# Orders of a step on four queues: normalising ahead of W's parts, squares and root ahead of the last parts of x1, statistics ahead of low parts, all quarter loads on SyncE

## The reference, cut to what matters

```python
# L0: adapter with layernorm, weights picked by language id
h = relu(x @ W1[lang] + b1[lang])            # 512x512 @ 512x128
y = x + h @ W2[lang] + b2[lang]              # 512x128 @ 128x512
mean = jnp.mean(y, axis=-1, keepdims=True)
var = jnp.mean(jnp.square(y - mean), axis=-1, keepdims=True)
normed = (y - mean) * jax.lax.rsqrt(var + LN_EPS)
x1 = x + normed * gamma[lang] + beta[lang]
# L1: linear, weights picked by category id
out = x1 + x1 @ W[cat] + b[cat]              # 512x512 @ 512x512
```

## Time and profile before

| | |
|---|---|
| median of 3 runs | 616.76 us |
| profiled execution, its own time | 616.09 us |
| its span | 614.3 us |
| TensorE busy | 607.1 us, 99% |
| VectorE, ScalarE, GpSimd busy | 523.2, 512.8, 524.0 us |
| HBM read and written | 132.17 and 33.55 MB |
| granted TensorE clock | 1.0 |

### The profile page before, as it was taken

One profiled execution on the slowest core, in us unless ns is written; L12 is line 12 of the kernel. 1 busy time (PEld: TensorE's weight loads), 2 busy tenths in 40 slices (PEclk: granted clock), 3 DMA queues, 4 the chain that ended last, 5 costly groups with the idle time before them and its releaser, 6 DMA issues.

```text
span 614.3 us, 10766 instructions
## 1 busy us (share of the span) xinstructions
PE 607.1 (99%) x2888; PEld 492.3 (80%) x2888; DVE 523.2 (85%) x1154; ACT 512.8 (83%) x769; POOL 524.0 (85%) x262
## 2 busy tenths in 40 slices
PE   9999999999999999999999999999999999999998
PEld 7767888888877888888888888888888888888887
DVE  1799899889799898898988998888898988998673
ACT  4768889889888889888989889889888989889770
POOL 4789999899889899889999888898988999888830
PEclk9999999999999999999999999999999999999999
DMA  9968998897997988989888998988998888998422
GB/s 308 247 206 272 307 305 275 278 296 250 307 297 251 301 271 281 318 270 292 274 287 280 306 297 258 287 280 273 313 290 280 281 287 275 300 306 276 154 85 104
DMA packets 125759, 166.24 MB, mean 271 GB/s; under 512 B 10882, under 2 KB 72588, under 8 KB 121632
## 3 DMA queue, kind: packets, MB, share of 16 engines
q1 hardware_dynamic: 94756, 150.12, 75.2%
q10 hardware_dynamic: 30972, 15.78, 9.2%
HBM read 132.17 MB, written 33.55 MB: 270 GB/s over the span
## 4 chain that ended last, share of the span: by engine, by line
PE 93%; DMA 2%; ACT 2%; DVE 2%; issue 1%; SPq 0%; POOL 0%; DVEq 0%; POOLq 0%; ACTq 0%
PE o_bank L828 18%; PE o_bank L830 18%; PE o_bank L829 18%; PE n_bank L846 9%; PE d_bank L828 5%; PE d_bank L830 5%; PE d_bank L829 5%; PE d_bank L859 5%; PE y_bank L828 2%; PE y_bank L830 2%; PE y_bank L829 2%; DMA x_tok<-in_x 2%; ACT norm L491 1%; PE y_bank L836 1%; DVE xT L659 1%
## 5 line engine op out<-in xcount | busy, mean ns | idle before, releaser
L828 PE MATMUL o_bank<-w_hi,x1T_hi 128*128 128x512 f32 x512 | 205.3, 401 | 0.8 <-DVE x1T_lo L724 0.8
L830 PE MATMUL o_bank<-w_hi,x1T_lo 128*128 128x512 f32 x512 | 200.0, 391 | 0.0
L829 PE MATMUL o_bank<-w_lo,x1T_hi 128*128 128x512 f32 x512 | 199.1, 389 | 0.0
L418 POOL TENSOR_TENSOR w_lo<-w_raw,w_hi 128x1024 fp32r<-128x1024 f32 x62 | 149.4, 2409 | 9.9 <-ACT w_hi L501 9.9
L659 DVE STREAM_TRANSPOSE xT<-x_quad 128x512 f32<-128x512 f32 x120 | 127.2, 1106 | 31.1 <-DMA x_quad<-in_x 31.1
L491 ACT ACTIVATE norm<-y,neg_mean_rstd,rstd 128x512 f32<-128x512 f32 x127 | 151.1, 1264 | 1.1 <-DVE neg_mean_rstd L709 1.1
L413 POOL TENSOR_TENSOR x_tok<-x_tok,b_bc 128x1024 f32<-128x1024 f32 x60 | 145.4, 2424 | 1.2 <-issue 1.1
L830 PEld LDWEIGHTS o_bank<-w_hi,x1T_lo 128*128 128x128 f32 x512 | 96.1, 188 | 21.0
L508 ACT ACTIVATE x1T_hi<-n_bank,params 128x512 fp32r<-128x512 f32 x126 | 84.6, 689 | 33.6 <-DVE n_bank L718 26.4
L828 PEld LDWEIGHTS o_bank<-w_hi,x1T_hi 128*128 128x128 f32 x512 | 96.3, 188 | 19.6 <-issue 1.7
L829 PEld LDWEIGHTS o_bank<-w_lo,x1T_hi 128*128 128x128 f32 x512 | 96.4, 188 | 17.8
(11 more groups left out here) (87 smaller groups left out, 821.2 us busy)
## 6 DMA issues: line engine op xcount, KB each, us to landing
w_raw<-in_L_cond_W SPq DMA_DIRECT2D x32, 1024.0 KB, 6.5
out<-out_half SPq DMA_DIRECT2D x63, 512.0 KB, 4.1
x_tok<-in_x SPq DMA_DIRECT2D x31, 1024.0 KB, 11.3
w_raw<-in_L_cond_W SPq DMA_DIRECT2D x64, 256.0 KB, 4.1
b_bc<-in_L_cond_b SPq DMA_DIRECT2D x64, 256.0 KB, 8.5
x_quad<-in_x SPq DMA_DIRECT2D x62, 256.0 KB, 3.7
x_quad<-in_x ACTq DMA_DIRECT2D x58, 256.0 KB, 10.7
x_tok<-in_x ACTq DMA_DIRECT2D x2, 256.0 KB, 3.3
```

The costliest lines, as they stand in the source:

```text
L418: pool.tensor_tensor(w_lo[q][:, c:c + 2, :], w_raw[q][:, c:c + 2, :], w_hi[q][:, c:c + 2, :].bitcast(F32), ALU.subtract).then_inc(w_lo_don ...
L828: pe.matmul(acc, lhs_hi, rhs_hi, start=first, stop=False)
L829: pe.matmul(acc, lhs_hi, rhs_lo, start=False, stop=False)
L830: return pe.matmul(acc, lhs_lo, rhs_hi, start=False, stop=last)
```

## The change

The order of the lists changes on four queues, and one issuer changes. No amount of arithmetic or of data changes.

- ScalarE: three of the four `normalise` now stand ahead of `high_w(k, 0)`, and the fourth ahead of `high_w(k, 2)`. W2's high part moves ahead of `relu`. The high parts of x and W1 of the next sample move from behind `high_x1` 0 and 1 to ahead of them. The fourth square and the root move ahead of `high_x1` 2 and 3. The DMA issue of two quarters goes.
- VectorE: `variance` and `inverse_deviation` move ahead of `low_x1` 2 and 3.
- GpSimd: the first sum with b2 moves ahead of `plus_identity`, the second ahead of the first low part of W; the low part of x stands ahead of that of W1.
- SyncE: all four quarters are loaded here. The parameters of sample k, not k+1, are now copied in step k, behind the load of x, and half 1 of sample k-3 is stored there.

```diff
 # SyncE, step
+                if w_load and k.since(2):
+                    lang_now = sample_id(0, k.sample(0), L)
                 if quads:
                     sp.wait_ge(xT_done, k.count(NC, 0, NC))
                     load_x_quads(k.sample(-2), p)
...
                 if loads:
                     load_b2(lang, q)
                     load_x(k.sample(-1), q)
+                if w_load and k.since(2):
+                    sp.wait_ge(x1_lo_done, k.count(NC, 1, 0))
+                    load_params(lang_now, p)
+                if linear and k.since(3):
+                    store(k, 3, 1)
                 if turn:
...
                     load_b(cat_b, q)
                 if linear:
                     store(k, 2, 0)
-                if loads:
-                    sp.wait_ge(x1_lo_done, k.count(NC, 0, 0))
-                    load_params(lang, q)
-                if linear:
-                    store(k, 2, 1)
 # GpSimd, step
+                    if adapter and not k.last(2):
+                        plus_b2_pair(0)
                     if turn:
                         plus_identity()
-                    if adapter:
+                    if adapter and k.last(2):
                         plus_b2_pair(0)
-                    if turn:
-                        low_w_pair(0)
                     if adapter:
                         plus_b2_pair(2)
                     if turn:
+                        low_w_pair(0)
                         low_w_pair(2)
                 if follow:
                     low_w2(q, k.count(1, -1, 1))
                     if k.since(2):
+                        low_xs(k)
                         low_w1(k)
-                        low_xs(k)
 # ScalarE, step
-                    high_w(k, 0)
-                    for t in range(NT):
-                        normalise(k, t)
+                for t in range(NT - 1):
+                    normalise(k, t)
+                high_w(k, 0)
+                normalise(k, NT - 1)
                 high_w(k, 2)
+                if follow:
+                    high_w2_of_next(k)
                 if adapter:
                     relu(k)
-                if follow and not k.last(S - 2):
-                    load_next_x_quads(k)
+                if follow:
+                    high_xs_of_next(k)
+                    high_w1_of_next(k)
                 high_x1(k, 0)
                 high_x1(k, 1)
-                if follow:
-                    high_w2_of_next(k)
-                    high_w1_of_next(k)
-                    high_xs_of_next(k)
                 if adapter:
-                    square(k, 0)
-                    square(k, 1)
-                    square(k, 2)
+                    for t in range(NT):
+                        square(k, t)
+                    deviation(k)
                 high_x1(k, 2)
                 high_x1(k, 3)
-                if adapter:
-                    square(k, 3)
-                    deviation(k)
 # VectorE, step
                 x1(k, 2)
                 x1(k, 3)
+                if adapter:
+                    variance(k)
+                    inverse_deviation(k)
                 low_x1(k, 2)
                 low_x1(k, 3)
                 output(k, 3)
-                if adapter:
-                    variance(k)
-                    inverse_deviation(k)
```

More of the change, by code:

```diff
@@ L234, in sample_id, with load_x_quads @@
                 return sp.value_load(ids[0:1, which, bass.ds(s, 1)], min_val=0, max_val=count - 1)
-            def load_x_quads(s, p, quads=(0, 1)):
-                for n in quads:
+            def load_x_quads(s, p):
+                for n in range(NQ):
                     sp.dma_start(x_quad[p][quad(n), :, :],
@@ L336, in _ @@
             load_params(lang1, 1)
-            load_x_quads(2, 0, range(NQ))
+            load_x_quads(2, 0)
             step(0, 1, linear=False)
@@ L350, in _ @@
             last = Step(S // ROUND, 3)
+            store(last, 3, 1)
             store(last, 2, 0)
@@ L547, in step @@
                 k = Step(h, p)
-                if k.last(2):
-                    for t in range(NT):
-                        normalise(k, t)
-                    high_w(k, 0)
-                else:
-                    high_w(k, 0)
-                    for t in range(NT):
-                        normalise(k, t)
+                for t in range(NT - 1):
+                    normalise(k, t)
+                high_w(k, 0)
+                normalise(k, NT - 1)
                 high_w(k, 2)
+                if follow:
+                    high_w2_of_next(k)
                 if adapter:
                     relu(k)
-                if follow and not k.last(S - 2):
-                    load_next_x_quads(k)
+                if follow:
+                    high_xs_of_next(k)
+                    high_w1_of_next(k)
                 high_x1(k, 0)
                 high_x1(k, 1)
-                if follow:
-                    high_w2_of_next(k)
-                    high_w1_of_next(k)
-                    high_xs_of_next(k)
                 if adapter:
-                    square(k, 0)
-                    square(k, 1)
-                    square(k, 2)
+                    for t in range(NT):
+                        square(k, t)
+                    deviation(k)
                 high_x1(k, 2)
                 high_x1(k, 3)
-                if adapter:
-                    square(k, 3)
-                    deviation(k)
-            def load_x_quads(s, p):
-                for n in (2, 3):
-                    act.dma_start(x_quad[p][quad(n), :, :],
-                                  x_quads[bass.ds(s, 1), n].rearrange("o j b f -> j (o b) f")
-                                  ).then_inc(xq_in[p], 16)
-            def load_next_x_quads(k):
-                act.wait_ge(xT_done, k.count(NC, 0, NC))
-                load_x_quads(k.sample(-2), k.b)
             act.dma_start(x_tok[0][:, 1, :], x_rows[0, :, 1, :]).then_inc(first_x_in[1], 16)
@@ L627, in _ @@
             high_w2_of_next(k1)
-            load_next_x_quads(k1)
             for p in range(2, 2 + ROUND):
```

## The result

The changed kernel takes 751.11 us (median of 4 runs, 748.37 to 754.19) against 616.63 us of the kernel before on the same chip: a ratio of 1.2173, 95% interval 1.2149 to 1.2197. The profiled execution took 749.55 us, its span is 747.7 us. Forecast were 711 us in a range of 675 to 750: the sign and the mechanism came out, the size did not.

A forecast was written before the change was run, and what follows sets the result against it. TensorE bound the old kernel; the copy behind SyncE's loads would set a 21.3 us period. relu(3) at 77.0, 27 periods, a 19.7 step, 36.6 to the end: 708.4; plus 1.8 is 710.5, said as 711 us, range 675 to 750.

The forecast's parts named there:

- the landing term of loop B: SyncE's queue, W1's issue to x landed: 2.88 MB at 319 GB/s plus 1.9 us, 10.9 us (bounds 10.1 to 13.4).
- loop B: relu, squares, SyncE's loads, parameters landing behind x, next relu: period 21.3 us (20.5 to 23.8), deciding; chance 0.84.
- The fixed part of the term: SyncE's loads: landing time beyond bytes over rate, 1.9 us, the middle of 2.3 and 1.5.
- the undiscounted row of 13.4 us: Kernel before: x landed 13.4 us behind W1's issue while about 1.05 MB of quarters moved; taken as upper bound.
- rival 1: SyncE: the small copy passes the loads or the queue isn't served in order; only loop A, 659.5 us; chance 0.10.
- Loop A: ScalarE and VectorE: low part of chunk 2 ready at 12.4 behind relu, due 11.1; period 19.7 us.
- Where TensorE waits: TensorE waits 2.9 us in each step, partly at down for hT_lo, mostly at chunk 2.
- rival 2: TensorE's clock falls in the waits; 923 us if half of each step ran at 1.2 GHz; chance 0.04.
- The rest, costed at nothing: ScalarE's norms and W parts, GpSimd's order, quarter loads and half 1's store fit within the longer step, adding nothing.
- rival 3: Hand-over to linear tile 0: chunk 2's low part stays within 1.1 us slack, copy not late; 615 us; chance 0.02.

The follow-up runs named there:

- h1: The changed kernel with W loaded by four DMAs of 128x512 in pieces of 2 KB instead of one with 8 KB pieces: 755.05 us.
- e9: The kernel before with one change, all four quarters of x issued by SyncE and none by ScalarE: 626.77 us, ratio 1.0171.
- g1: The changed kernel with the parameter copy directly behind W1 and W2 and the store of half 1 behind it, both ahead of W, b2 and x: 654.85 us.
- e10: The kernel before with three normalise ahead of W's parts and GpSimd's order of the change: 633.48 us, ratio 1.0277.
- e6: The kernel before with squares, root and statistics ahead of the last high and low parts of x1: 643.34 us, ratio 1.0439.
- e5: The kernel before with the high parts of the next W2, W1 and x ahead of the first two high parts of x1: 680.69 us, ratio 1.1047.
- f1: The changed kernel with the parameter copy directly behind the loads of W1 and W2, the half store left in place: 667.37 us, ratio 1.0814.
- g2: g1's kernel with the high parts of the next x and W1 back behind the first two high parts of x1: 629.65 us, ratio 1.0215.
- h2: The changed kernel with W's load issued ahead of the wait for the squares and of W1's load: 686.17 us, ratio 1.1119.

## Why the prediction was wrong in size and right in kind

**The failed step is the landing term of loop B,** "How long from the issue of W1 until x has landed", 10.9 us = 2.88 MB at 319 GB/s plus 1.9. Measured are 12.4 on average and 13.4 in the step shown (383.24 to 396.6), inside the bounds that I gave (10.1 to 13.4). From relu(3) at 77.20 to relu(30) at 691.47 are 27 turns of 22.75, where 21.3 was forecast. 27 times 1.45 us is 39 us, and 710.5 + 39 = 749.5 is the profiled execution; the other terms cancel to within half a microsecond.

The fixed part of the term, 1.9 us, held: W1 lands 2.7 behind its issue, just as 0.26 MB at 319 GB/s and 1.9 us give. What failed is the one rate for all that follows. W and b2 took 6.1 us for the 4.1 that it gives them, and x 2.7 for its 3.3. I took the mean rate from a stretch in which another issuer's quarters kept the DMA engines full; in the changed kernel the queue is empty when W1 is issued. Why W and b2 are slow there stays open. The form of W is excluded by h1, and both are fast in e9.

**The range failed with it.** Its upper end, 750, allowed 1.4 us more a step, a landing of 12.3; the mean was 12.4. I had set aside the undiscounted row of 13.4 us, in which x landed behind W1 in the kernel before. It would have forecast a turn of 23.8, too long by 1 us.

**Loop B as a mechanism:** right. relu(2) at 53.88 (55.7 forecast), relu(3) at 77.20 (77.0; luck, since a start 1.8 us too late and a turn 2.0 too short met), from relu(31) to the end 36.7 (36.6), squares done and W1 issued 10.27 behind relu (10.3). The queue serves in order, which rival 1 denied: the copy lands 0.3 us behind x, and in 1.7 us when only W1 and W2 stand ahead. The section "Queues, rings and completion order" of the Trainium skill, "DMA: Bandwidth & Descriptors", says the same of a ring; the trace agrees with 10.7 us against 3.0.

**Loop A:** right, but loop B covers it in this kernel up to the last turn, relu(30) to relu(31), 19.52 us. g1 shows it in all steps: 19.56 us a step (19.7), chunk 2 taken 12.25 behind relu (12.4), 654.85 us for the kernel with nothing else in its way.

**Where TensorE waits:** I said mostly at chunk 2. It waits 1.85 at down and 0.59 at chunk 2. The period isn't touched by that, only by relu.

**The clock (rival 2)** fell, and cost nothing where a run can show it. Behind the wait of 1.85 us at down the windows read 0.63 and 0.52, the lower of the two levels for most of the time, and a matmul of 128x512 takes 0.43 us instead of 0.23. But the first square comes 7.07 behind relu in this kernel and 7.08 in g1 (342.49 to 349.57), where the clock is 1.00 in that stretch. So that distance didn't feel the fall; it shows in the busy time, 643.4 against 607.1. It doesn't come in each step that waits: the clock record of this trace has 13 such falls between relu(3) and relu(31). In step 2, with the longest wait, the clock stood at the lower level for ten microseconds:

```profile
50.00:58.00 8.00, 2.04 (x5) 1.66 (x6) 1.79 (x3) 4.08 (x6) 1.38 (x1) 0.50 1.12 336
```

The Trainium skill, "TensorE: Matmul & The Clock Gate", Part 1, says that an idle array falls to half rate; in step 2 and in the step shown it did, and over the execution the mean granted clock is 0.963.

**The rest, costed at nothing:** true in this kernel, since loop B and loop A leave the room, but for a weaker reason than I gave. I looked at the busy time of ScalarE per step, not at what each moved instruction waits for. The single orders cost 1.7% to 10.5% in the old kernel (e9, e10, e6, e5), and the trace of each has a new wait of the moved or the following instruction.

**"No loss" (rival 3)** has no support. The best of the eighteen variants is 1.7% slower than the kernel before.

## What to carry to other kernels

A kernel whose bound engine is 99% busy can hide several loops that are only a microsecond or so shorter; before moving an instruction, follow it around its whole loop, through every queue and back, and not only up to the bound engine. A small transfer that is needed soon must not stand on a queue behind megabytes; ahead of W, b2 and x relu never waited for it, though the store behind them then had to be moved as well (f1, g1). When a landing has to be forecast behind a burst, read the landing of each transfer of the like burst by itself, and ask what stood on the queue ahead of it: here neither the mean rate with a fixed part (10.9) nor the like row taken whole (13.4) gave the 12.4. Orders that were found together have to be tested together: norm first and statistics first were each slower alone than the kernel of g2 with both.

## What was not expected of the hardware

A queue that had been empty moved nothing for one microsecond, 287 GB/s for two, 262 and 213 in the next six and then 381, with the same issuer and all loads and the copy issued within 2.6 us. The same loads behind quarters in e9 had no such stretch. In h2, with W1 and W2 and then only b2 ahead of x, the queue read 89 GB/s for three microseconds, while in e9 b2 landed 0.7 us behind W. TensorE's granted clock read 0.63 and 0.52 behind a wait of 1.85 us and 1.00 again from 380 us on.
